# Choosing the experts from logits instead of probabilities, and another order of the work in the last attention group

## The reference

```python
h = gelu(ri @ r1_w.T + r1_b)                  # 128 hidden units per token
probs = softmax(h @ r2_w.T, -1)               # 32 experts
topp, topi = top_k(probs, 2)
wnorm = topp / topp.sum(-1, keepdims=True)    # weights of the two chosen
hit = topi[..., None] == arange(32)
score = where(hit.any(1), probs, -inf)        # per expert, the best 140 tokens by score
idx = argsort(-score, axis=0)[:cap].T
```

## Time and profile before

| | us |
|---|---|
| median of 3 runs | 742.74 |
| the three runs | 739.95, 742.74, 744.35 |
| the profiled execution | 735.4 |
| its span | 733.6 |
| TensorE busy in the span | 642.9 (88%) |
| VectorE busy in the span | 504.8 (69%) |

### The profile page before, as it was taken

The page is one execution under the profiler, slowest core; times in us unless marked ns, Lnnn a source line. Parts: engine busy times, 40 slices in busy tenths (PEclk is TensorE's granted clock), DMA queues, the critical chain, the costliest instruction groups (busy, mean ns, idle before and its releaser), DMA issues.

```text
span 733.6 us, 17667 instructions
## 1 busy us (share of the span) xinstructions
PE 642.9 (88%) x5322; PEld 512.5 (70%) x5322; DVE 504.8 (69%) x1718; ACT 414.5 (56%) x1644; POOL 330.0 (45%) x340
## 2 busy tenths in 40 slices
PE   7898999998999989999777217999999999999992
PEld 4565666665666666667555104999999999999992
DVE  6866877868788687876988797658666865732230
ACT  2497888878888888886764344423432433222320
POOL 3435371744637256271202004256655566556643
PEclk9799999999999999999987556999999999999996
DMA  5511200112021020100002411588888888888821
GB/s 189 208 56 27 78 27 26 52 28 75 26 59 42 2 75 26 50 0 26 27 1 81 166 26 35 148 253 260 237 256 247 235 263 231 240 261 268 268 37 17
DMA packets 57864, 84.94 MB, mean 116 GB/s; under 512 B 11581, under 2 KB 28597, under 8 KB 57781
## 3 DMA queue, kind: packets, MB, share of 16 engines
q1 hardware_dynamic: 47588, 73.34, 31.0%
q0 software_dynamic: 9216, 9.76, 7.9%
q10 hardware_dynamic: 976, 0.89, 0.4%
HBM read 71.28 MB, written 12.69 MB: 114 GB/s over the span
## 4 chain that ended last, share of the span: by engine, by line
PE 50%; DVE 14%; POOL 10%; issue 7%; ACT 7%; DMA 3%; DVEq 0%; POOLq 0%; ACTq 0%
PE pair L1066 16%; PE bank L1076 8%; PE pair L1712 4%; ACT arena L1384 4%; PE pair L1721 4%; PE pair L519 2%; PE bank L1660 2%; DMA arena<-rows,slot_row 2%; DVE arena L622 2%; PE bank L1673 2%; PE pair L1707 2%; PE bank L1738 2%; POOL arena L1230 2%; POOL rows_out L940 2%; POOL arena L1239 2%
## 5 line engine op out<-in xcount | busy, mean ns | idle before, releaser
L1384 ACT ACTIVATE arena<-pair,arena 112x112 f32<-112x112 f32 x512 | 174.0, 377 | 12.1 <-DVE arena L1542 11.9
L1066 PE MATMUL pair<-arena,we 128*128 128x140 f32 x1024 | 142.1, 286 | 1.0 <-ACT arena L962 1.0
L940 POOL DMA_INDIRECT rows_out<-arena,slot_row x64 | 96.1, 1502 | 102.5 <-DVE arena L997 86.5
L1066 PEld LDWEIGHTS pair<-arena,we 128*128 128x128 f32 x1024 | 129.2, 190 | 1.1 <-issue 1.1
L970 ACT ACTIVATE arena<-pair 128x140 f32<-128x140 f32 x160 | 46.0, 288 | 141.9 <-PE pair L1066 141.9
L1384 ACT ACTIVATION_READ_ACCUMULATOR arena<-pair,arena 112x1 f32 x512 | 116.4, 227 | 0.0
L1542 DVE TENSOR_REDUCE arena<-pair 112x8 f32<-112x896 f32 x64 | 69.8, 1091 | 53.1 <-PE pair L1712 50.6
L929 POOL DMA_INDIRECT arena<-rows,slot_row x64 | 63.2, 987 | 68.4 <-issue 67.1
L1012 DVE TENSOR_TENSOR arena<-arena,pair 128x140 f32<-128x140 f32 x128 | 37.8, 296 | 70.3 <-ACT arena L970 68.2
L1076 PE MATMUL bank<-arena,we 128*128 128x140 f32 x512 | 83.3, 286 | 0.0
L1721 PE MATMUL pair<-tab,arena 112*112 112x112 f32 x512 | 68.3, 273 | 7.0 <-ACT arena L1384 6.6
(11 more groups left out here) (198 smaller groups left out, 1214.5 us busy)
## 6 DMA issues: line engine op xcount, KB each, us to landing
we<-w_experts_in SPq DMA_DIRECT2D x192, 256.0 KB, 4.1
wa<-w_adapters_in SPq DMA_DIRECT2D x16, 384.0 KB, 6.1
arena<-ctx_in SPq DMA_DIRECT2D x8, 448.0 KB, 4.4
arena<-x_in SPq DMA_DIRECT2D x8, 448.0 KB, 4.1
rows_out<-arena SPq DMA_DIRECT2D x8, 448.0 KB, 3.3
rows<-arena SPq DMA_DIRECT2D x8, 448.0 KB, 3.4
arena<-rows,slot_row POOLq DMA_INDIRECT x64, 4.1
rows_out<-arena,slot_row POOLq DMA_INDIRECT x64
```

The source lines that it names most:

```text
L940: nc.gpsimd.indirect_dma_start(d["out"], bass.IndirectOffsetOnAxis(ap=slot_row[:, h, e:e + 1], axis=0), yr[e % 2][:, h, :], None, compute_ ...
L1066: last = nc.tensor.matmul(banks[m % 4][:, part * CAP:(part + 1) * CAP], w[:, col0:col0 + 128], xet[j % 2][:, c, :], start=(c == 0), stop=( ...
L1384: last = nc.scalar.activation(pr[s % 2][:, j, :], banks[BS[s % 4]][0:T, j * T:(j + 1) * T], ACT.Exp, bias=nmx[s // 2 % 2][:, s % 2, j:j + ...
```

## The change

The experts are chosen from the logits. A chunk's `shift_logits` now takes the eight greatest logits of each row straight from PSUM (`max`, once for each row), instead of the maximum alone. With the second greatest known, the comparison needs no probabilities, so one of the two `max` passes of `choose` is gone, and the sum, reciprocal and probabilities come last. The weight of a token is made from the exponential of the difference of its two greatest logits, which ScalarE takes in one more small instruction. The tables are rewritten: the logits of the first chunk are made in one piece at step 4, its exponential is taken at step 5 and not 6, nothing of the choice stands on VectorE in steps 8 to 12, the second chunk is shifted at step 13 and not 9, the parts after it are put elsewhere. The hidden layer of group 6 is held on ScalarE from step 15 to step 19 (`HIDDEN_LAST`). In the tail `keep_warm` goes from 24 to 17 products at step 23 and from 7 to 5 at step 28, and `HIDDEN_ROWS` moves from the tail's step 13 to 12.

```diff
-IDLE = {7: 24, 12: 7, 14: 2}
+IDLE = {7: 17, 12: 5, 14: 2}
...
-LOGITS = {4: (0, 1), 5: (2, 3), 9: (4, 5), 20: (6,)}
+LOGITS = {4: (0, 1, 2, 3), 9: (4, 5), 20: (6,)}
...
-SHIFTED, RAISED = (5, 9, 22), (6, 10, 22)
-PARTS = 9
-CHOOSE = {7: ((0, 0), (0, 1)), 8: ((0, 2),), 11: ((0, 3), (0, 4)), 13: ((0, 5),), 15: ((0, 6), (1, 0), (1, 1)),
-          16: ((0, 7), (0, 8)), 18: ((1, 2),), 19: ((1, 3),), 20: ((1, 4),), 22: ((1, 5), (1, 6)),
-          29: ((1, 7), (1, 8)), 30: tuple((2, part) for part in range(PARTS))}
-
-HIDDEN_ROWS, HIDDEN_BANK = 13, 1
+SHIFTED, RAISED = (5, 13, 22), (5, 14, 22)
+PARTS = 8
+CHOOSE = {7: ((0, 0), (0, 1)), 13: ((0, 2), (0, 3)), 15: ((0, 4), (0, 5), (0, 6), (0, 7)), 19: ((1, 0), (1, 1), (1, 2)),
+          29: tuple((1, part) for part in range(3, PARTS)),
+          30: tuple((2, part) for part in range(PARTS))}
+
+HIDDEN_ROWS, HIDDEN_BANK = 12, 1
+HIDDEN_LAST = 3
...
-            nc.scalar.activation(w0[:, rows, :], w0[:, rows, :], ACT.Exp).then_inc(s_e, 1)
+            nc.scalar.activation(prb[:, rows, :], w0[:, rows, :], ACT.Exp).then_inc(s_e, 1)
+            nc.scalar.activation(col[4][:, rows], col[0][:, rows], ACT.Exp).then_inc(s_e2, 1)
...
-        link(nc.vector.tensor_reduce(col[0][:, rows], lg, X, ALU.max))
-        link(nc.vector.tensor_tensor(w0[:, rows, :], lg, over_e(col[0][:, rows]), ALU.subtract))
+        for b in range(n):
+            last = nc.vector.max(top8[:, rows.start + b, :], lg[:, b, :])
+        link(last)
+        nc.vector.tensor_tensor(col[0][:, rows], top8[:, rows, 1], top8[:, rows, 0], ALU.subtract)
+        link(nc.vector.tensor_tensor(w0[:, rows, :], lg, over_e(top8[:, rows, 0]), ALU.subtract))
...
         if part == 0:
+            link(nc.vector.tensor_tensor(v, u, over_e(c[0]), ALU.subtract))
+        elif part == 1:
             dve.wait_ge(s_e, count)
-            link(nc.vector.tensor_reduce(c[1], u, X, ALU.add))
+            link(nc.vector.scalar_tensor_tensor(u, v, 0.0, over_b(tab[0:T, TAB["rev"]], n), ALU.is_ge, ALU.mult))
+        elif part == 2:
+            link(nc.vector.scalar_tensor_tensor(u, v, 0.0, u, ALU.is_gt, ALU.add))
+        elif part == 3:
+            for b in range(rows.start, rows.stop):
+                last = nc.vector.max(key8[:, b, :], w0[:, b, :])
+            link(last)
+        elif part == 4:
+            link(nc.vector.tensor_tensor(v, u, over_e(key8[:, rows, 1]), ALU.is_ge))
+        elif part == 5:
+            link(nc.vector.tensor_reduce(c[1], p, X, ALU.add))
             link(nc.vector.reciprocal(c[2], c[1]))
-        elif part == 1:
-            link(nc.vector.tensor_tensor(p, u, over_e(c[2]), ALU.mult))
-        elif part in (2, 6):
-            values, out = (prb, top8) if part == 2 else (w0, key8)
-            for b in range(rows.start, rows.stop):
-                last = nc.vector.max(out[:, b, :], values[:, b, :])
-            link(last)
-        elif part == 3:
-            link(nc.vector.tensor_tensor(v, p, second(top8), ALU.subtract))
-        elif part == 4:
-            link(nc.vector.scalar_tensor_tensor(u, v, 0.0, over_b(tab[0:T, TAB["rev"]], n), ALU.is_ge, ALU.mult))
-        elif part == 5:
-            link(nc.vector.scalar_tensor_tensor(u, v, 0.0, u, ALU.is_gt, ALU.add))
+        elif part == 6:
+            link(nc.vector.tensor_tensor(p, p, over_e(c[2]), ALU.mult))
         elif part == 7:
...
-            link(nc.vector.tensor_tensor(col[0], top8[:, :, 0], top8[:, :, 1], ALU.add))
+            link(nc.vector.scalar_tensor_tensor(col[0], col[4], 1.0, col[2], ALU.add, ALU.mult))
...
+                held = own and not front and what == "H"
+                if (what not in "VO") and not held and (own and (what, j) in EARLY_ITEMS) == early:
...
+                if not own and prev and s == HIDDEN_LAST:
+                    kind, n = 2, len(ROUTE) - 1
+                    item(g - 2, par, kind, "H", 0, n, False, False)
```

More of the change, by code:

```diff
@@ L412, in program @@
     sc = [take(T, [PER, LCH, GROUP]) for _ in range(LISTS)]
-    col = [take(T, [NB]) for _ in range(4)]
+    col = [take(T, [NB]) for _ in range(5)]
     assert used[0] <= free_early
@@ L706, in choose @@
         p, u, v = (a[:, rows, :] for a in (prb, w0, w1))
-        second = lambda a: over_e(a[:, rows, 1])
         if part == 0:
+            link(nc.vector.tensor_tensor(v, u, over_e(c[0]), ALU.subtract))
+        elif part == 1:
             dve.wait_ge(s_e, count)
-            link(nc.vector.tensor_reduce(c[1], u, X, ALU.add))
-            link(nc.vector.reciprocal(c[2], c[1]))
-        elif part == 1:
-            link(nc.vector.tensor_tensor(p, u, over_e(c[2]), ALU.mult))
-        elif part in (2, 6):
-            values, out = (prb, top8) if part == 2 else (w0, key8)
-            for b in range(rows.start, rows.stop):
-                last = nc.vector.max(out[:, b, :], values[:, b, :])
-            link(last)
-        elif part == 3:
-            link(nc.vector.tensor_tensor(v, p, second(top8), ALU.subtract))
-        elif part == 4:
-            link(nc.vector.scalar_tensor_tensor(u, v, 0.0, over_b(tab[0:T, TAB["rev"]], n), ALU.is_ge, ALU.mult))
-        elif part == 5:
-            link(nc.vector.scalar_tensor_tensor(u, v, 0.0, u, ALU.is_gt, ALU.add))
+            link(nc.vector.scalar_tensor_tensor(u, v, 0.0, over_b(tab[0:T, TAB["rev"]], n), ALU.is_ge, ALU.mult))
[9 more added lines that the diff above has]
+            link(nc.vector.tensor_reduce(c[1], p, X, ALU.add))
+            link(nc.vector.reciprocal(c[2], c[1]))
+        elif part == 6:
+            link(nc.vector.tensor_tensor(p, p, over_e(c[2]), ALU.mult))
         elif part == 7:
-            link(nc.vector.tensor_tensor(v, u, second(key8), ALU.is_ge))
-        elif part == 8:
             by_chunk = lambda a: a.rearrange("p (c j) e -> p c j e", j=PER)
@@ L767, in routing_vector @@
         rows_stored(dve)
+        dve.wait_ge(s_e2, len(EARLY_ROWS) + 1)
         def beside(n):
@@ L1350, in items @@
             for kind, back, what, j, n in at_step(s, 0, front, own, prev):
-                if (what not in "VO") and (own and (what, j) in EARLY_ITEMS) == early:
+                held = own and not front and what == "H"
+                if (what not in "VO") and not held and (own and (what, j) in EARLY_ITEMS) == early:
                     item(g - back, (par + back) % 2, kind, what, j, n, front and not own, not front and not own)
```

1 line of the change is left out of this document (added).

## The result

The changed kernel takes 735.48 us (median of 11 runs, 730.88 to 737.63), the kernel before beside it 740.17 us (11 runs, 734.18 to 746.92). The ratio is 0.9936, with a 95% interval of 0.9908 to 0.9964: 4.7 us faster (2.7 to 6.8), where 3.6 were forecast. The two profiled executions, though, take nearly the same: 736.66 us (span 734.9) after, 735.4 (span 733.6) before. So the first thing to read is where this one execution of the changed kernel lost what the medians show.

The account below looks back on a forecast made before the run. VectorE's chain was taken to bound the last group and tail: last scores 3.7 us early, less 0.2 for PSUM, 3.5, taken as 3.6 us; 739.1 us against the 742.74 median, own range 737 to 741, whole range 734 to 744.

Parts of the forecast that it names:

- rival 2: TensorE's clock: closer-packed work avoids half clock at 384.0 to 390.5 us; gain up to 6.9 us, 735.8; chance 0.16.
- the small subtraction: VectorE's subtraction of 16 numbers in the shift: taken as 0.1 us, bounds 0 and 0.25 us.
- rival 1: `max` from PSUM is dear: gain only 0.7 to 1.7 us, time 741 to 742; chance 0.12.
- Step 5: First logits in one piece: VectorE's shift starts at 345.25 us, 0.9 us sooner, and ends as before at 347.75.
- Steps 5 to 7: ScalarE's copy queues behind the exponential's wait, VectorE's scaling 0.6 us late; given back by step 8, 353.06 against 353.00 us.
- Steps 8 to 10: 16 `max` and the second chunk's shift leave VectorE: step 10's maximum at 359.1 us, 2.5 us early.
- Step 12: Scores need GpSimd's keys, ending at 361.48 us; the maximum starts at 363.2 instead of 366.29 us, 3.1 us early.
- Steps 14 to the last scores: Step 14's 2.07 us idle time filled, maximum at 370.7 us; layer norm 383.6, last shift 397.5, scores 401.7, 3.7 us early.
- The hold of the hidden layer: ScalarE's hidden layer, held to step 19, ends by 380.3 us and costs nothing; without that cover up to 0.6 us.
- PSUM: 28 new `max` on the path read PSUM: 0.007 us more each, 0.2 us in all; 1.8 us by the skill's rule.
- Rivals 3 and 4: Third: early VectorE time isn't passed on, 742, chance 0.08. Fourth: slower through the clock, up to 747, chance 0.06.
- Rival 4: With fewer unread products TensorE stays at half clock from step 22 through the tail: scores 1.1 us late; chance 0.06.

Follow-up runs that it names:

- keys first: Changed kernel with GpSimd making the last group's selection keys of the fourth batch ahead of the router's statistics, not behind: 734.51 us, ratio 0.9935.
- 24 unread products: Changed kernel with 24 and 7 unread products in the tail, as before, instead of 17 and 5: 735.28 us, ratio 0.9938.
- split logits: Changed kernel with the first chunk's logits in two pieces again, at steps 4 and 5: 736.62 us, ratio 0.9963.
- remedy: Changed kernel with six more unread products at steps 6 and 8 (734.61 us), ScalarE's copy ahead of the exponentials (733.65), or that copy plus other changes (733.95).
- the 1.12: Microseconds taken off VectorE in the tail: changed kernel with the probabilities' product and two chunks' scores on GpSimd; 734.89 us, ratio 0.9953.

## Why the prediction was right, and where not

**The sum.** Forecast 3.6 us against the kernel before, measured 4.7 (2.7 to 6.8). By the traces the stretch from step 4's maximum to the last scores, 65.2 and 65.7 us before, is 64.5, 62.8 and 62.1 us in three kernels that share the choice and the tables (changed, keys first, 24 unread products): 0.7 to 3.6 us shorter, depending on where the clock fell. The forecast's 61.5 is reached only where it didn't fall in steps 5 to 9. The rest of the 4.7 isn't traced; it lies within the interval. That the total came so near is in part luck: the forecast had no term for the clock, which took 2 us and more from the chain in step 10, while the runs as a whole had a higher mean clock than those of before (rival 2 below). The absolute forecast, 739.1 us in a range of its own of 737 to 741, was not met: 735.48. It rested on a median of three runs of the kernel before, 742.74, where eleven give 740.17; from that it would have been 736.6. Two small slips are in the working. The 3.5 us were raised to 3.6 for the small subtraction, but that takes 0.11 us to the next instruction (348.85 to 348.96 us), just the 0.1 already in it; and the 1.7 us of rival 1 has the cost of PSUM in it twice, 3.7 - 1.8 is 1.9.

**Step 5** (shift at 345.25, 5.1 us after the maximum): 4.95. This was right; by the trace with the split logits it is worth what was said. **Steps 5 to 7** (scaling 0.6 us late, given back): with the clock at 1.00 it is 0.35 us late and given back on VectorE, step 8 begins at 12.6 us, before at 12.8. What the step missed is TensorE, which idles behind the same copy.

**Steps 8 to 10** (maximum 2.5 us early, "no wait"): the step that failed. Its mechanism, VectorE's freed time, is right, since 18.1 to 18.5 us come out with the clock kept, and 18.9 was forecast. But in the changed kernel it is 22.6, and it waits 1.95 to 2.68 us for the scores in all seven profiles without a remedy, because a half-clock stretch of TensorE's, in the kernel before at 363.8 to 370.5 us and at 384 to 390.9, now falls in steps 5 to 9. I had weighed the clock for the tail alone (rivals 2 and 4).

**Step 12** (held by GpSimd's keys, 23.0): right as a mechanism, 1.66 us against 1.67 from keys to maximum, but hidden in the changed kernel by the wait two steps earlier.

**Steps 14 to the last scores** (31.0 us, 370.7 to 401.7): 31.1 in the changed kernel, 406.73 - 375.62. The idle time of step 14 is filled, the layer norm waits for GpSimd's root (0.60 us), the last shift waits for no logits, and the time from the last scores to the end is 328.2 us in both profiles (327.7 in the second one of before). All of this was right. The hold of the hidden layer was put at no cost, and at up to 0.6 us without it: 0.55, and 0.9 more that goes with the clock of that execution.

**PSUM.** Rival 1 is out: 16 `max` take 1.67 us from PSUM and 1.59 from SBUF (lines 700 and 722 above), 5 ns each, forecast 7. The rule of the Trainium skill (Perfetto Trace Analysis, "Optimizing Scalar/DVE Operations"), 60 ns of overhead on SBUF against 125 on PSUM, doesn't show in these rows, and the measurement decides.

**Rival 2**, more gain through the clock: the stretch of 384.0 to 390.5 us is at 1.00 now, as this rival had it, but another took its place earlier, and the net isn't a gain in the profiled execution. It isn't out, though. The mean granted clock is 0.9424 over the changed kernel's eleven runs and 0.9376 over 108 of the kernel before; at the 5.7 us for 0.01 that the last section fits, that goes with 2.7 of the 4.7 us, and by the changed kernel's own fit (3.9 us) with 1.9. Since a time and its clock are only seen together, this doesn't say which is the cause: about half of the gain may be this rival's, and no experiment parts the two. **Rivals 3 and 4** are out by the interval. Rival 4's premise came true without its consequence: in the profile without the hold TensorE ran the unread products at half clock, and the stretch from the layer norm to the last scores is 18.29 us there, 18.27 in the changed kernel.

## What to carry to other kernels

Work taken off the engine that bounds is worth its full time only up to the next wait. After each such step, read which engine was idle behind the same semaphore. Here TensorE's idling of 0.5 and 0.3 us went ahead of a half-clock stretch, and that made VectorE wait 2.68 us. Compare places between two traces from a common event ahead of the change, not from the start of the span, and don't judge a change of half a per cent by one profiled execution of each. Removing and adding work on a bounding engine are two tests: here adding cost at least the work, and removing gave nothing where a second chain lay just behind.

## What the runs showed of the hardware

Over 108 executions of the kernel before, time and mean granted clock go together: the correlation is -0.87, with a fitted 5.7 us for each 0.01 of clock, and the clocks of the 11 or 12 runs of each other kernel go with their times in the same way (-0.74 to -0.93). So most of the scatter of one kernel, 733.8 to 746.5 us, goes with how much of it TensorE spends at its lower level. The traces show these stretches at other places in each execution: in the loop none in the first profile of before between 36 and 340 us, in the second at 64 to 72 and 272 to 276.

In the changed kernel's profile the clock fell at about 347.5 us with TensorE busy throughout from 340 us (5.00 of 5.00 and 2.50 of 2.50 us); the kernel with the tables alone did the same at 347.4 us (7.00 of 7.00 us busy from 340). In the other profiles with these tables it fell after visible idling. So busy time alone didn't tell when it falls. In both of those executions the 32 narrow logits products stood just ahead (3.24 us from 343.78 in the changed kernel). They can't be enough: the other kernels with these products in one piece kept 1.00 for at least 4 us behind them, and with the products in two pieces the clock fell 5 us later all the same.

VectorE's operation with two 112x128 inputs took 0.59 us beside GpSimd's product of two 112x256 inputs (0.70 us from 398.19), and 0.29 us in the changed kernel. The Trainium skill (SBUF — State Buffer, "SBUF: two separate sides") has a VectorE operation with two SBUF inputs and a GpSimd operation that reads SBUF take one port pair by an exclusive lock. This row roughly fits it; one row doesn't tell a lock from sharing. The 0.30 us is the largest part of the 0.5 us that the tail didn't keep of the 1.12.
